# Moving the SBUF buffers of a two-stage retention and mixture-of-experts kernel to multiples of 1 KB

## The reference, cut to what matters

```
x: [32, 512, 256]                       # batches, tokens, channels; all float32
xn = layernorm(x)
q, k, v = xn @ Wq + bq, xn @ Wk + bk, xn @ Wv + bv      # 16 heads of 16
out = ((q k^T) * mask) v  per head      # mask[i,j] = 0.95 ** (i - j) for i >= j
out = out @ Wo + bo; group norm over (16 channels x 512 tokens), gamma, beta
probs = softmax(xn @ gate_w)            # [32, 512, 8 experts]
top_p, top_idx = top_k over the tokens of each (batch, expert), 128 of 512
h = gelu(xn[top_idx] @ w1[e]); y = (h @ w2[e]) * top_p  # w1: 256x1024, w2: 1024x256
result = x + out + scatter_add(y at top_idx)
```

## Time and profile before

| what | value |
|---|---|
| median of 3 runs | 2335.57 us |
| the profiled execution's own time | 2340.57 us |
| its span, first to last instruction | 2338.6 us |
| instructions | 81411 |
| DMA | 157.72 MB, mean 67 GB/s |

### The profile page before, as it was taken

One profiled execution on the slowest core, in us unless ns is written; L12 is line 12 of the kernel. 1 busy time (PEld: TensorE's weight loads), 2 busy tenths in 40 slices (PEclk: granted clock), 3 DMA queues, 4 the chain that ended last, 5 costly groups with the idle time before them and its releaser, 6 DMA issues.

```text
span 2338.6 us, 81411 instructions
## 1 busy us (share of the span) xinstructions
PE 2264.5 (97%) x34252; PEld 2095.6 (90%) x34252; DVE 1531.5 (65%) x3103; ACT 1391.5 (59%) x2553; POOL 1283.3 (55%) x2012
## 2 busy tenths in 40 slices
PE   6999999999999988999999999999999999999998
PEld 5777777777777778999999999999999999999998
DVE  3555555656666657996766767667667667676674
ACT  4555565555655546556666656666666666666664
POOL 4444444444544455655566666666566576575453
PEclk9999999999999999999999999999999999999999
DMA  3232222322223312232324324224234233232332
GB/s 120 74 95 85 75 76 83 94 84 76 76 75 94 98 61 71 49 77 50 50 44 89 46 46 91 43 49 86 47 52 82 47 54 80 48 54 43 51 50 33
DMA packets 129368, 157.72 MB, mean 67 GB/s; under 512 B 11008, under 2 KB 118656, under 8 KB 129024
## 3 DMA queue, kind: packets, MB, share of 16 engines
q0 software_dynamic: 49152, 67.14, 17.8%
q1 hardware_dynamic: 79872, 85.54, 11.6%
HBM read 85.53 MB, written 67.11 MB: 65 GB/s over the span
## 4 chain that ended last, share of the span: by engine, by line
PE 55%; DVE 0%; POOL 0%; issue 0%; ACT 0%; DVEq 0%
PE attn L1779 28%; PE scores L1698 18%; PE front L1698 7%; PE front L1688 2%; POOL out L798 0%; DVE rows L211 0%; DVE topi L207 0%; DVE top L202 0%; DVE hidden L1263 0%; DVE xs_lo L1233 0%; ACT res L949 0%; DVE rows L223 0%; PE scores L233 0%; PE scores L232 0%; DVE rows L225 0%
## 5 line engine op out<-in xcount | busy, mean ns | idle before, releaser
L1779 PE MATMUL attn<-w_hi,g_hi 128*128 128x256 f32 x2048 | 581.5, 284 | 2.5 <-DVE g_lo L1274 2.4
L1779 PE MATMUL attn<-w_lo,g_hi 128*128 128x256 f32 x2048 | 578.3, 282 | 0.0
L1779 PE MATMUL attn<-w_hi,g_lo 128*128 128x256 f32 x2048 | 578.1, 282 | 0.0
L987 ACT ACTIVATE hidden<-hidden 128x512 f32<-128x512 f32 x384 | 235.4, 629 | 263.9 <-DVE hidden L1263 263.9
L1779 PEld LDWEIGHTS attn<-w_hi,g_hi 128*128 128x128 f32 x2048 | 388.6, 190 | 3.0 <-DVE g_lo L1274 2.7
L1779 PEld LDWEIGHTS attn<-w_hi,g_lo 128*128 128x128 f32 x2048 | 388.3, 190 | 0.0
L1779 PEld LDWEIGHTS attn<-w_lo,g_hi 128*128 128x128 f32 x2048 | 388.0, 189 | 0.0
L1698 PE MATMUL scores<-xs_hi,w_hi 128*128 128x256 f32 x1280 | 362.0, 283 | 8.4 <-DVE xs_lo L1233 6.3
L1698 PE MATMUL scores<-xs_lo,w_hi 128*128 128x256 f32 x1280 | 362.8, 283 | 0.0
L1263 DVE TENSOR_TENSOR hidden<-front,hidden 128x512 f32<-128x512 f32 x256 | 176.3, 689 | 284.0 <-PE front L1698 270.7
L1698 PE MATMUL scores<-xs_hi,w_lo 128*128 128x256 f32 x1280 | 361.0, 282 | 0.0
(11 more groups left out here) (182 smaller groups left out, 5154.4 us busy)
## 6 DMA issues: line engine op xcount, KB each, us to landing
x<-in_x SPq DMA_DIRECT2D x32, 512.0 KB, 5.3
w_stage<-in_w SPq DMA_DIRECT2D x16, 1024.0 KB, 6.4
xn_rows<-xn SPq DMA_DIRECT2D x32, 512.0 KB, 3.2
res<-in_x SPq DMA_DIRECT2D x32, 512.0 KB, 3.8
out<-res SPq DMA_DIRECT2D x32, 512.0 KB, 3.4
xg<-xn_rows,step_idx POOLq DMA_INDIRECT x256
out<-y,scatter_idx POOLq DMA_INDIRECT x128, 3.9
out<-res,scatter_idx POOLq DMA_INDIRECT x128, 3.9
```

Of the source, the lines that this page charges most:

```text
L987: act.activation(own(q, p), src, ACT.Gelu).then_inc(g_ready, 1)
L1779: last = pe.matmul(yb[k % 2][:, 0:D], g_[:, m, cols], w, start=start and m == first and i == 0, stop=end, skip_group_check=True)
```

## The change

No instruction, wait or order is changed; only start addresses are. The small statistics and index buffers are allocated ahead of the others (which moves the softmax, top-k, `w1_stage` and `res` buffers up by 768 bytes), and the large buffers behind `res` get written offsets, most of them multiples of 1 KB. `v_unbiased` lies behind `vg_hi` (remainder 128), the states and the second `v_parity` are packed against a neighbour (remainders 512, 256 and 512).

```diff
         cst = sb("cst", [P, C_N])
         vec = sb("vec", [P, V_N])
+        gst_w = sb("gate_stage", [P, DH, E])
+        st = sb("ln_stats", [P, TT, 6])
+        mv = sb("ln_mv", [P, TT, 2])
...
+        idx = sb("step_idx", [P, GRP], U32)
+        sidx = sb("scatter_idx", [P, GRP], U32)
         route = Routing(ctx, nc, cst)
...
-        w_hi = [None if i == 2 else sb(f"w_hi{i}", [P, DH, D], F32R) for i in range(4)]
-        w_lo = [sb(f"w_lo{i}", [P, DH, D], F32R) for i in range(4)]
-        vg_hi = sb("vg_hi", [P, DH, VG], F32R)
...
-        x_hi = sb("x_hi", [P, DH, S], F32R)
-        x_lo = sb("x_lo", [P, DH, S], F32R)
+        KB = 1024
+        bv = at("bv_rows", [P, D], F32, 53 * KB)
+        w_hi = [None if i == 2 else at(f"w_hi{i}", [P, DH, D], F32R, o * KB)
+                for i, o in enumerate((54, 56, None, 58))]
+        w_lo = [at(f"w_lo{i}", [P, DH, D], F32R, (60 + 2 * i) * KB) for i in range(4)]
+        xb = [at(f"x{i}", [P, TT, D], F32, (68 + 4 * i) * KB) for i in range(2)]
+        xn = at("xn", [P, TT, D], F32, 76 * KB)
+        vg_hi = at("vg_hi", [P, DH, VG], F32R, 80 * KB)
+        vraw = at("v_unbiased", [P, TT, VG], F32, 80 * KB + DH * VG * 4)
...
+        x_hi = at("x_hi", [P, DH, S], F32R, 90 * KB)
+        x_lo = at("x_lo", [P, DH, S], F32R, 94 * KB)
...
-        LATE = 186880
-        w1h = [at("w1_hi0", [P, 7, QF], F32R, LATE), at("w1_hi1", [P, 7, QF], F32R, 56448)]
-        w1l = [at("w1_lo0", [P, 7, QF], F32R, LATE + K1), at("w1_lo1", [P, 7, QF], F32R, 167584)]
...
+        w1h = [at("w1_hi0", [P, 7, QF], F32R, 183 * KB), at("w1_hi1", [P, 7, QF], F32R, 57 * KB)]
+        w1l = [at("w1_lo0", [P, 7, QF], F32R, 197 * KB), at("w1_lo1", [P, 7, QF], F32R, 165 * KB)]
+        s2 = at("w2_stage", [P, FT, D], F32, 211 * KB)
+        w2h = [at("w2_hi0", [P, FT, D], F32R, 79 * KB), at("w2_hi1", [P, FT, D], F32R, 105 * KB)]
...
+        xs_hi = at("xs_hi", [P, 7, HALF], F32R, 87 * KB)
+        xs_lo = at("xs_lo", [P, 7, HALF], F32R, 94 * KB)
...
+        g_hi = at("g_hi", [P, FT, SL], F32R, 133 * KB)
+        g_lo = at("g_lo", [P, FT, SL], F32R, 149 * KB)
```

More of the change, by code:

```diff
@@ L254, in layer @@
         vec = sb("vec", [P, V_N])
+        gst_w = sb("gate_stage", [P, DH, E])
+        st = sb("ln_stats", [P, TT, 6])
+        mv = sb("ln_mv", [P, TT, 2])
+        ln_ve, ln_r, ln_y, ln_a, ln_m = (sb(f"ln_{n}", [P, TT]) for n in ("ve", "r", "y", "a", "m"))
+        ost = sb("o_stats", [P, DH, 6])
+        gm = sb("g_moments", [P, DH, 2])
+        gs = sb("g_means", [P, DH, 2])
+        gn_ve, gn_r, gn_y, gn_a, gn_m, gn_s, gn_b = (sb(f"gn_{n}", [P, DH])
+                                                     for n in ("ve", "r", "y", "a", "m", "s", "b"))
+        idx = sb("step_idx", [P, GRP], U32)
+        sidx = sb("scatter_idx", [P, GRP], U32)
         route = Routing(ctx, nc, cst)
@@ L261, in layer @@
         wst = s1[:, 0:4, :].rearrange("p a (b n) -> p (a b) n", n=D).rearrange("p (i h) n -> p i h n", h=DH)
-        gst_w = sb("gate_stage", [P, DH, E])
-        bv = sb("bv_rows", [P, D])
-        w_hi = [None if i == 2 else sb(f"w_hi{i}", [P, DH, D], F32R) for i in range(4)]
-        w_lo = [sb(f"w_lo{i}", [P, DH, D], F32R) for i in range(4)]
-        vg_hi = sb("vg_hi", [P, DH, VG], F32R)
-        xb = [sb(f"x{i}", [P, TT, D]) for i in range(2)]
-        xn = sb("xn", [P, TT, D])
-        vraw = sb("v_unbiased", [P, TT, VG])
@@ L271, in layer @@
-        st = sb("ln_stats", [P, TT, 6])
-        mv = sb("ln_mv", [P, TT, 2])
-        ln_ve, ln_r, ln_y, ln_a, ln_m = (sb(f"ln_{n}", [P, TT]) for n in ("ve", "r", "y", "a", "m"))
-        x_hi = sb("x_hi", [P, DH, S], F32R)
-        x_lo = sb("x_lo", [P, DH, S], F32R)
[L276 to L289, removed]
@@ L290, in layer @@
-        gn_ve, gn_r, gn_y, gn_a, gn_m, gn_s, gn_b = (sb(f"gn_{n}", [P, DH])
-                                                     for n in ("ve", "r", "y", "a", "m", "s", "b"))
+        KB = 1024
[4 more added lines that the diff above has]
+        xb = [at(f"x{i}", [P, TT, D], F32, (68 + 4 * i) * KB) for i in range(2)]
@@ new lines, in layer @@
+        xn = at("xn", [P, TT, D], F32, 76 * KB)
+        vg_hi = at("vg_hi", [P, DH, VG], F32R, 80 * KB)
+        vraw = at("v_unbiased", [P, TT, VG], F32, 80 * KB + DH * VG * 4)
+        tm = [at(f"state{i}", [P, NSUB - 1, DH, 2 * HD], F32, 90 * KB - (2 - i) * (NSUB - 1) * DH * 2 * HD * 4)
+              for i in range(2)]
+        x_hi = at("x_hi", [P, DH, S], F32R, 90 * KB)
+        x_lo = at("x_lo", [P, DH, S], F32R, 94 * KB)
+        q32 = at("q32", [P, DH, S], F32, 98 * KB)
+        qm = [at(f"q_parity{i}", [P, DH, 2, S], F32, (102 + 8 * i) * KB) for i in range(2)]
@@ new lines, in layer @@
+        qd = [at(f"q_decayed{i}", [P, DH, S], F32, (118 + 4 * i) * KB) for i in range(2)]
+        k32 = [at(f"k{i}", [P, DH, S], F32, (126 + 4 * i) * KB) for i in range(2)]
+        kn = at("k_natural", [P, TT, D], F32, 134 * KB)
+        vm = [at(f"v_parity{i}", [P, TT, VW], F32, 138 * KB + i * TT * VW * 4) for i in range(2)]
+        s_sb = [at(f"s_sb{i}", [P, PAIRS, 512], F32, (155 + 8 * i) * KB) for i in range(2)]
+        a_hi = at("a_hi", [P, DH, S], F32R, 171 * KB)
+        a_lo = at("a_lo", [P, DH, S], F32R, 175 * KB)
@@ L293, in layer @@
+        o32 = at("o32", [P, DH, S], F32, 179 * KB)
         tb = ctx.enter_context(nc.psum_tensor("front", [P, DH, 512], F32))
@@ L382, in layer @@
         HALF = SL // 2
-        K1 = 7 * QF * 4
-        K2 = FT * D * 4
-        KX = 7 * HALF * 4
-        LATE = 186880
-        w1h = [at("w1_hi0", [P, 7, QF], F32R, LATE), at("w1_hi1", [P, 7, QF], F32R, 56448)]
-        w1l = [at("w1_lo0", [P, 7, QF], F32R, LATE + K1), at("w1_lo1", [P, 7, QF], F32R, 167584)]
[L389 to L400, removed]
@@ L401, in layer @@
-        y = [at("y", [P, GRP, D], F32, 126624), res]
-        g_hi = at("g_hi", [P, FT, SL], F32R, 134816)
-        g_lo = at("g_lo", [P, FT, SL], F32R, 151200)
+        w1h = [at("w1_hi0", [P, 7, QF], F32R, 183 * KB), at("w1_hi1", [P, 7, QF], F32R, 57 * KB)]
+        w1l = [at("w1_lo0", [P, 7, QF], F32R, 197 * KB), at("w1_lo1", [P, 7, QF], F32R, 165 * KB)]
+        s2 = at("w2_stage", [P, FT, D], F32, 211 * KB)
+        w2h = [at("w2_hi0", [P, FT, D], F32R, 79 * KB), at("w2_hi1", [P, FT, D], F32R, 105 * KB)]
@@ new lines, in layer @@
+        w2l = [[at(f"w2_lo{i}{j}", [P, FT // 2, D], F32R, o * KB) for j, o in enumerate(os)]
+               for i, os in enumerate(((71, 75), (179, 219)))]
+        xg = [at(f"xg{k}", [P, D], F32, (53 + k) * KB) for k in range(GRP)]
+        xs_hi = at("xs_hi", [P, 7, HALF], F32R, 87 * KB)
+        xs_lo = at("xs_lo", [P, 7, HALF], F32R, 94 * KB)
+        xsum = at("x_sums", [P, 4, HALF], F32, 101 * KB)
+        hid = {q: at(f"hidden{q}", [P, 2, 2, HALF], F32, o * KB)
+               for q, o in (("22", 113), ("21", 117), ("11", 121), ("12", 129))}
@@ L405, in layer @@
+        y = [at("y", [P, GRP, D], F32, 125 * KB), res]
+        g_hi = at("g_hi", [P, FT, SL], F32R, 133 * KB)
+        g_lo = at("g_lo", [P, FT, SL], F32R, 149 * KB)
         xb_ = {p: sbk[:, i, :] for i, p in enumerate("AB")}
```

## The result

The kernel after takes 2349.30 us, the median of 6 runs (2344.98 to 2351.66), against 2335.61 us for the kernel before, also of 6 (2334.29 to 2340.81). The ratio is 1.0049, with a 95% interval of 1.0033 to 1.0065: slower by 13.7 us, which is beyond the 7 us that a measurement can tell from no change. The forecast was no change; what came is rival 2, with 2351 us named for it. The predicted range of 2309 to 2355 holds the time, because it was drawn over most of the rivals and not because the forecast came near.

What follows compares the result with a forecast made beforehand. The prediction took PE, busy for 97% of the span, to bound the kernel. All terms were 0: 2340.6 + 0 us profiled, 5.0 above the median, so 2335.6, named as 2335 us, with an 8-in-10 range of 2309 to 2355.

Steps and rivals of the forecast that it cites:

- rival 2: Stage 2: weight loads with the same remainder as the stream beside them slow matmuls, 16 us, to 2351 us; chance 0.25.
- What bounds the kernel: PE, busy for 97% of the span; time is the number of matmuls by the distance between their starts.
- instructions, waits and queues at 0: Whole kernel: no instruction, wait or queue entry is added, removed or moved; 0 us.
- ACT, DVE, POOL and DMAs at 0: Other engines and transfers: address effects within 1% on the engines, hidden beside PE's work; 0 us.
- Equal even and odd steps: Stage 2: even and odd experts' steps become equal, within 0.1 us of 22.23 us each.
- Stage 2's matmuls at 0: 11,520 matmuls: 0 us, the middle between all steps like even ones (-4.9 us) and all like odd ones (+4.9 us).
- rival 1: Stage 2, some in stage 1: operands not off by 32 bytes stream faster; 18 us, to 2318 us; chance 0.29.
- Stage 1 at 0: Stage 1's matmuls: loss goes with the columns, 2.6 us at 0.84 ns either way; taken as 0 us.
- Rival 3: Stage 2 and more in stage 1: unaligned layout keeps PE from full rate; 127 us, about 2200 us; chance 0.03.
- The rules weighed: SBUF's 16-byte-line rule made the change worth exactly 0; the trace's even and odd steps disagreed by 0.15 us a step.

Runs made afterwards that it cites:

- all_plus_32: The kernel after with every written offset moved 32 bytes higher; 2348.40 us in one run.
- both_sets_64_128: The kernel after with weights moved so that, in both sets, down-projections have phase 64 and up-projections 128; 2312.99 us, ratio to before 0.9902.
- w_plus_32_96: The kernel after with g_hi and g_lo moved by 32 bytes and the even set's w1 by 96; 2332.55 us in one run.
- w_plus_192_256: The kernel after with g_hi and g_lo moved by 192 bytes and the even set's w1 by 256; 2326.78 us in one run.
- w_plus_64_128: The kernel after with g_hi and g_lo moved by 64 bytes and the even set's w1 by 128; 2321.89 us in one run.
- w_plus_320_384: The kernel after with g_hi and g_lo moved by 320 bytes and the even set's w1 by 384; 2322.90 us in one run.
- all_at_64_stage1: The kernel after with all stage 2 matmuls at phase 64, and stage 1's projections too (w_hi, w_lo, bv_rows down by 192); 2326.70 us, ratio to before 0.9961.

## Why the prediction was wrong

*What bounds the kernel, and instructions, waits and queues at 0:* right. The same 34252 matmuls, no wait late, and the whole of the change in the distance between starts.

*ACT, DVE, POOL and DMAs at 0:* right. The means above moved by up to 1%, and all of it lies beside PE's work.

*Equal even and odd steps, "the surest part":* right, to 0.01 us in a window of 112.30.

*Stage 2's matmuls at 0:* this is the step that failed. With the phase of every load at 0 a steady step became 0.24 us longer, 1.3 ns for each of 180 matmuls, and 55 steady steps alone came out at +13.3 us. The term was 0, and its ends of -4.9 and +4.9 were too near. Two things went wrong. First, the ends were taken as the even and the odd pace of 22.154 and 22.306 us, though both are means over operands with different remainders; a mixture says little about a layout in which all are the same. Odd down-projections were the nearest row, 119.2 ns over matmuls of which only most shared their remainder. In the trace of the kernel before, the odd down-projections of the second half, whose loads all have phase 0 (the rows on `w2_hi1` and `w2_lo10`), already settle at 120 ns from start to start. Second, the middle was taken between this row and one that had less of the new layout. The rule should have been to follow the trait that all of the new matmuls share, which was the equal remainder. A smaller slip: 117.5 ns for even up-projections is one piece of 12, and over all their pieces the trace has 118.1, so the price of a stationary operand in rival 1 was read too wide as well.

*Rival 2:* right in place, sign and size. It wanted steps above 22.34 us (22.46 came), 119 to 121 ns (120.0), 16 us (13.7). The traces bear out the place it named, too. In the odd window of the kernel before, the distance from an `xs_lo,w_hi` matmul to the next is 121.2 ns (mean of 140), and beside this one the piece of `w1_lo1` with the equal remainder is loaded; the distances from the other two kinds are 118.3 and 117.4. The `xs_hi,w_lo` matmul, which has that equal remainder to its own stationary operand, is the one with 117.4, so it is the load beside the stream that counts. Two points of it were off. The period is 256 bytes, not 512: its example of a mean of 284 against 281 ns holds for either. And "longer means of all three kinds of matmul" holds for two: stage 1's became shorter. Its counter-argument, that odd `w_hi,g_hi` matmuls show no excess beyond 0.9 ns, was no argument against it. The 0.9 ns was the effect itself, in part of the matmuls.

*Stage 1 at 0, with 2.6 us either way:* not refuted by the stage's length, for the 3.1 us lie within the variation told above. But the reading behind it, that the loss goes with the columns, holds only for the kernel before (234 ns, about twice 118). At phase 0 it fails: L1381's distance fell to 228.5 ns while that of 256 columns rose to 120.0. By 1152 matmuls this is 6 us less work for PE, which the windows show (788.3 against 794.3 us busy).

*Rival 1:* refuted by all_plus_32. What looked like an effect of multiples of 64 in the even and odd steps was one of phase. *Rival 3:* 113.3 ns is the best pace of stage 2's matmuls in any run, and 1.31 us for a piece of 12 never came. The 109 ns that rival 3 set beside it is what the section it cites, of the Trainium skill (TensorE: Matmul & The Clock Gate, Back-to-back issue gap), calls the isolated gap, and not that of a stream of loads and matmuls. That the layout before kept PE from a better pace was true, though: a third of the 11 ns is to be had, by the phases, and by other offsets than those of the change.

*The rules weighed.* By the Trainium skill (SBUF — State Buffer, Specifications), that lines are of 16 bytes and only crossings cost, every kernel of this study would take the same time. The runs disagree by 51 us. They also go against a sentence that the prediction left aside, from the Trainium skill (TensorE: Matmul & The Clock Gate, Part 2: What happens when you issue a matmul): "Loading the next tile's weights doesn't steal SBUF read bandwidth from the running matmul." The loads of both_sets_64_128 and of the kernel after are the same in number and size and differ only in where they lie, and a step takes 21.91 and 22.46 us. That it is bandwidth which is lost isn't shown.

**What stays open.** That two read streams meet in the same part of SBUF would explain why their distance matters, but no run shows it. Not shown either is what switches between the two paces at phase 64, why 160 is as slow as 0, why 512 columns prefer phase 0, and whether the region of SBUF counts besides (0.06 us a step is left open by w_plus_32_96).

## What to carry to other kernels

Where TensorE is busy without a gap, divide the pieces of the chain by their counts, and compare steps that do the same work on other buffers: a difference there is the price of addresses. Then look at the distance between the stationary piece that is loaded and the moving row beside it, modulo 256 bytes, rather than at round offsets; multiples of 1 KB for all put every pair at distance 0, which with 160 was the slowest seen here for 256 columns, and the fastest of three for 512. As the best layout isn't predictable from these runs, try several: each is an edit of a few offsets.

## What was not expected of the hardware

- **120.0 ns at phase 0, exactly.** At 2.4 GHz that is 288 cycles for 256 columns, 32 more than the columns. For 512 columns the 248 distances between matmuls on `a_hi` and `a_lo` from 200 to 800 us have a mean of 226.7 ns, 544 cycles, again 32 more: at phase 0 the loss goes with the loads, not with the columns.
- **Two steady paces at one phase.** 117.8 and 113.3 ns (272 cycles, 16 more than the columns) at phase 64, each kept over whole pieces. Phase 192 shows both as well (w_plus_192_256).
- **How well it repeats.** Steps of different executions with equal phases agree to 0.01 us (22.46 in the kernel after and all_plus_32, 21.92 in w_plus_64_128 and w_plus_320_384), while whole executions of one kernel differ by up to 20 us (all_at_64_stage1, 2318.59 to 2338.30). A step's length tells more than several medians.
